# An attention layer on one core: the sum over head groups made in DRAM by accumulating transfers

## The chip, the cores and the metric

The kernel runs on one core of a Trainium2 chip. A core has TensorE (matrix products, written PE in the profile, its weight loads PEld), VectorE (DVE), ScalarE (ACT), GpSimd (POOL) and SyncE (SP), which here only issues transfers. The engines run on their own instruction streams and wait for each other through semaphores. SP and ACT issue transfers to hardware queues, GpSimd to a software queue; all of them are carried out by the same 16 DMA engines. The metric is the device time of one execution in microseconds (us).

## What is computed

```python
# x: (1, 2048, 512); 16 heads, q/k of 128+64, v of 128; latent of 384 for q, 128 for k and v
def attn(x, w_qa, q_ln, w_qb, w_kva, kv_ln, w_kvb, w_o):
    q = rms_norm(x @ w_qa.T, q_ln) @ w_qb.T        # per head: 128 plain, 64 rotated
    ckv = x @ w_kva.T                              # 128 latent, 64 rotated key part
    kv = rms_norm(ckv[..., :128], kv_ln) @ w_kvb.T
    scores = causal(q_full @ k_full.T * 192 ** -0.5)
    return merge_heads(softmax(scores) @ v) @ w_o.T
x = layernorm(x + attn(x, ...))
x = layernorm(x + x @ (weight * scale_weight[:, None]).T + bias)
```

## The kernel before

The program has three phases, with a barrier of all engines between them.

The **first phase** (up to 162 us) folds the weights, projects the tokens and leaves their latent forms in SBUF and DRAM. Its last transfer on the SP queue copies the input `x` into a DRAM tensor `y_dram` of 16 tiles (128 tokens by 512 outputs each). So `y_dram` starts as the residual, and the attention phase adds the attention's output to it.

The **attention phase** (162 to 1811 us) runs over 64 turns, numbered `it`: 4 groups of 4 heads (`G`), and in each group the 16 tiles of 128 queries, in the order of `PAIR_ORDER`. A turn of query tile `n` has `keys(it)` = n + 1 key tiles, from 1 to 16, together 544. For each key tile TensorE makes the scores of 4 heads (`scores`, 5 products), ScalarE copies them to a ring in SBUF (`copy_scores`), VectorE keeps the running maximum (`max_of`), later subtracts it (`shift`), ScalarE takes the exponent (`exp`) and its rounded part (`hi`), VectorE adds up the sum (`add_up`), GpSimd makes the rest of the split (`values_lo`, L1282), and TensorE multiplies with the values (`values`). After a turn's last key tile come the step of the sum (`turn_sum`, `reduce_sum`, `spread_sum`), `normalise` on VectorE, the split of the output into `o_t` (`out_hi` on ScalarE, `out_lo` on GpSimd, L1287) and the product with the group's part of the output weights (`project_out`, 12 products, L1148, semaphore `y_ready`). It leaves a tile of 128x512 in one of three shared PSUM banks.

This tile has to be added to `y_dram`. In the kernel before, SP loads the tile of `y_dram` into one of two halves of the SBUF tensor `y` (`load_y`, L959), VectorE adds the PSUM bank to it (`add_y`, L1338, semaphore `y_added`), and SP stores it (`store_y`, L963). Since each tile is summed once in each of the 4 groups, `next_y` makes the load of the next turn wait until the last store has landed (`y_stored`). The PSUM bank is free for the next use when the add is done (`wait_read`). At the end of a group SP also loads the next group's output weights (`wo`, L974), behind the store in its program.

The order of all steps is made ahead of time by `timetable()` and `plan()`. The timetable gives each step a slot (one slot is one key tile) and a phase inside it; `e` is the slot of a turn's last `values`, and `("y", it)` stands at slot e + 4. What reads a shared bank (`readers`) comes one slot later, in phase READ. `plan()` lists the steps in this order, pulls ahead what `waits_for` names, and every engine runs through the list and takes its own kinds of step. So an instruction that waits holds up all that stands behind it on its engine.

After the list, GpSimd issues the loads for the **last phase** (1811 to 1906 us): the second layer's weights (L1304, 1024 KB), their scales (L1305) and the first 10 of the 16 finished tiles of `y_dram` (L1309). Those 12 transfers stand ahead of the barrier; behind it SP loads the last 6 tiles (L1509) and GpSimd the bias (L1535, L1537). The last phase takes the statistics of each tile, normalises, multiplies by the second weights, adds the bias and residual, normalises again and writes the output.

Of the kernel before, what the change touches and what calls it, by code (L numbers as in the profile page):

```python
# [53 lines left out]
class Memory:  # L54


    def __init__(self, nc, ctx):
# [26 lines left out]

        self.y_stored = ctx.enter_context(nc.semaphore("y_stored"))
# [9 lines left out]
def prepare_phase(nc, m, x, w_qa, w_kva, w_qb, w_kvb, w_o, q_ln, kv_ln, ident_in, mask_in, cos_in, sin_in):  # L95
# [6 lines left out]
    with ExitStack() as ctx:  # L102
# [114 lines left out]
        def _(sp):  # L217
# [12 lines left out]
            sp.dma_start(m.y_dram.rearrange("t p d -> (t p) d"), x).then_inc(m.y_stored, 16)  # L230
# [412 lines left out]
def timetable():  # L643

    for it in range(N_ITER):
# [17 lines left out]
        yield e + 4, USE_AT, ("y", it)  # L663
    for it in range(-2, N_ITER - 2):
        ahead = [("q", it // 2 + 1, 2 * (it % 2) + j) for j in range(2)]
        following = [("pe", it + 3)] if it + 3 < N_ITER and not opens_group(it + 3) else []
        if opens_group(it + 2):
            order = [("pe", it + 2), *ahead, ("turn_pe", it + 2), *following]
        else:
            order = [("turn_pe", it + 2), *following, *ahead]  # L670
        for j, use in enumerate(order):
            yield (window_slot(it, min(j, 3)) if it >= 0 else it), USE_AT, use


def readers(use):
# [13 lines left out]
    if use[0] == "y":  # L689
        return [("add_y", use[1])]  # L690
# [14 lines left out]
def waits_for(step):  # L705
# [70 lines left out]
    elif what == "add_y":  # L776
        yield ("y", it)
    elif what == "q_hi":
# [76 lines left out]
def attention_phase(nc, m, w_ffn, scale_w):  # L855


    with ExitStack() as ctx:
# [30 lines left out]
        y_loaded = [sem(f"y_loaded{n}") for n in range(2)]  # L889
        y_stored = m.y_stored  # L890
        y_added = sem("y_added")
# [65 lines left out]
        def _(sp):  # L957
            def load_y(o):
                sp.dma_start(y[:, o % 2, :], m.y_dram[tile_of(o)]).then_inc(y_loaded[o % 2], 16)  # L959

            def store_y(o):
                sp.wait_ge(y_added, o + 1)
                sp.dma_start(m.y_dram[tile_of(o)], y[:, o % 2, :]).then_inc(y_stored, 16)  # L963

            def next_y(o):
                if o + 1 < N_ITER and tile_of(o + 1) != tile_of(o):
                    sp.wait_ge(y_stored, 16 * (o + 1))
                    load_y(o + 1)
                store_y(o)
                if o + 1 < N_ITER and tile_of(o + 1) == tile_of(o):  # L970
                    sp.wait_ge(y_stored, 16 * (o + 2))
                    load_y(o + 1)
                if o % NT == NT - 1 and o + 1 < N_ITER:
                    sp.dma_start(words(m.wo), m.wo_dram[group(o)]).then_inc(wo_loaded, 16)  # L974
# [21 lines left out]
            sp.wait_ge(y_stored, 16)  # L996
            load_y(0)
            load_tokens(1)
            for what, *at in STEPS:
                if what in ("q", "pe"):  # L1000
                    next_tokens((what, *at))
                elif what == "y":
                    next_y(*at)
            sp.wait_ge(y_stored, 16 * (N_ITER + 1))
# [5 lines left out]
        def _(pe):  # L1010
            def wait_read(u):
# [7 lines left out]
                elif u[0] == "y":  # L1019
                    pe.wait_ge(y_added, u[1] + 1)  # L1020
# [157 lines left out]
        def _(act):  # L1178
# [53 lines left out]

            def out_hi(it):
# [5 lines left out]
            for what, *at in STEPS:  # L1239
# [14 lines left out]
                elif what == "copy_sum":  # L1254
                    copy_sum(*at)
                elif what == "o_hi":
                    out_hi(*at)

        @block.gpsimd
        def _(pool):  # L1260
# [23 lines left out]

            def out_lo(it):
# [3 lines left out]

            for what, *at in STEPS:  # L1290
# [6 lines left out]
                elif what == "o_lo":  # L1297
                    out_lo(*at)

# [7 lines left out]
            pool.wait_ge(y_stored, 16 * (N_ITER - NT + Y_FIRST + 1))  # L1307
# [4 lines left out]
        def _(dve):  # L1312
# [21 lines left out]

            def add_y(it):
                dve.wait_ge(y_ready, it + 1)
                dve.wait_ge(y_loaded[it % 2], 16 * (it // 2 + 1))
                nc.vector.tensor_tensor(y[:, it % 2, :], aux(("y", it)), y[:, it % 2, :], ALU.add).then_inc(y_added, 1)  # L1338
# [63 lines left out]
            for what, *at in STEPS:  # L1402
# [4 lines left out]
                elif what == "add_y":  # L1407
                    add_y(*at)
# [301 lines left out]
```

## Time and profile before

| | |
|---|---|
| median of 3 runs | 1909.88 us (1907.77 to 1910.48) |
| the profiled execution | 1907.47 us |
| its span, first to last instruction | 1905.8 us |
| busy share of the span: TensorE | 92% |
| VectorE | 74% |
| ScalarE | 59% |
| GpSimd | 52% |
| mean DMA rate over the span | 66 GB/s |

The profile is of one execution. Its own time (1907.47 us) is 1.7 us over the span, for what lies around the first and the last instruction, and 2.4 us below the median of the runs; what is worked out from it is laid on the median at the end. A row of a timeline gives the start and the duration in us, the engine, the line of the program, the operation, output and inputs, and in brackets how long the engine had been idle and what released it. "SPq" and "POOLq" are the queues' own instructions. Busy shares are means over stages with different limits.

### The profile page before, as it was taken

To read this page: it belongs to the slowest core of one execution; us is meant where nothing else is said; L and a number is where in the kernel's file an instruction comes from. 1 tells how busy PE (TensorE), PEld (TensorE's weight loads), DVE (VectorE), ACT (ScalarE), POOL (GpSimd) and SP (SyncE) were. 2 spreads that over 40 slices of the span, in tenths; PEclk is the share of its full clock that TensorE was granted. 3 is DMA by queue.
4 is the path that set the end of the run, shared out by engine and by line. 5 is a ranking of instruction groups with operands and counts; after the bars stand their busy time and mean duration, and the time that the engine had idled before them with its cause. 6 is when DMAs were issued, how large, how long until landed. Compare 5 with 4: busy or idle time off the path is not lost. (4 is left out here: it accounts for less than half of the span.)

```text
span 1905.8 us, 28136 instructions
## 1 busy us (share of the span) xinstructions
PE 1756.6 (92%) x8977; PEld 1415.6 (74%) x8977; DVE 1401.1 (74%) x2659; ACT 1129.1 (59%) x2247; POOL 988.6 (52%) x971
## 2 busy tenths in 40 slices
PE   5997899999999999999989999999999999998586
PEld 3565788888878778788877788887787878886442
DVE  1553588787878778878777688878788888877266
ACT  2553366666666666667556566666667667666220
POOL 2321255555555555555555465655556656556455
PEclk9998999999999999999999999999999999999899
DMA  7774101111111201010211101111111010100321
GB/s 229 296 307 165 39 18 34 45 34 45 67 40 40 82 14 56 23 56 12 85 43 66 58 22 45 34 45 67 40 40 67 28 39 34 34 23 23 122 72 56
DMA packets 56488, 125.96 MB, mean 66 GB/s; under 512 B 8800, under 2 KB 30560, under 8 KB 53984
## 3 DMA queue, kind: packets, MB, share of 16 engines
q1 hardware_dynamic: 47776, 76.56, 11.8%
q0 software_dynamic: 6848, 23.60, 3.7%
q10 hardware_dynamic: 1728, 24.12, 3.0%
q8 instruction: 69, 1.13, 0.2%
q14 instruction: 67, 0.55, 0.1%
HBM read 79.17 MB, written 49.28 MB: 67 GB/s over the span
## 5 line engine op out<-in xcount | busy, mean ns | idle before, releaser
L1282 POOL TENSOR_TENSOR split_p<-pool,split_p 128x512 fp32r<-128x512 f32 x544 | 704.6, 1296 | 524.1 <-ACT split_p L1219 523.8
L1088 PE MATMUL rows<-q_c,key_c 128*128 128x512 f32 x1632 | 480.5, 402 | 15.4 <-DVE top L1357 7.9
L1357 DVE TENSOR_TENSOR top<-rows,top 128x512 f32<-128x512 f32 x420 | 288.6, 687 | 188.1 <-ACT pool L1207 184.0
L1372 DVE TENSOR_TENSOR pool<-bank,pool 128x512 f32<-128x512 f32 x544 | 370.4, 681 | 22.3 <-PE bank L1106 21.9
L1207 ACT COPY pool<-rows 128x512 f32<-128x512 f32 x480 | 282.6, 589 | 144.7 <-PE rows L1088 143.5
L1212 ACT ACTIVATE pool<-pool 128x512 f32<-128x512 f32 x544 | 346.8, 638 | 36.0 <-DVE pool L1372 34.9
L1088 PE MATMUL rows<-q_pe,key_pe 128*128 128x512 f32 x1088 | 337.8, 392 | 0.0
L1219 ACT CAST split_p<-pool 128x512 fp32r<-128x512 f32 x544 | 333.3, 613 | 0.0
L1384 DVE TENSOR_TENSOR bank<-bank,pool 128x512 f32<-128x512 f32 x480 | 331.1, 690 | 0.0
L1088 PEld LDWEIGHTS rows<-q_c,key_c 128*128 128x128 f32 x1632 | 282.2, 189 | 62.8 <-DVE top L1357 14.2
L1088 PEld LDWEIGHTS rows<-q_pe,key_pe 128*128 128x128 f32 x1088 | 204.3, 188 | 46.3
L1116 PE MATMUL bank<-split_p,val 128*128 128x512 f32 x544 | 214.9, 395 | 7.3 <-ACT o_sum L1225 6.0
L1119 PE MATMUL bank<-split_p,val 128*128 128x512 f32 x544 | 215.0, 395 | 3.6 <-POOL split_p L1282 3.4
L1117 PE MATMUL bank<-split_p,val 128*128 128x512 f32 x544 | 212.3, 390 | 0.0
L1148 PE MATMUL rows<-wo,o_t 128*128 128x512 f32 x516 | 130.1, 402 | 22.4 <-POOL o_t L1287 22.3
L1189 ACT CAST rot<-rot_cos 128x256 fp32r<-128x256 f32 x64 | 26.0, 406 | 192.8 <-POOL rot_cos L1271 192.8
L1148 PEld LDWEIGHTS rows<-wo,o_t 128*128 128x128 f32 x516 | 97.0, 192 | 51.9 <-issue 31.8
L1287 POOL TENSOR_TENSOR o_t<-o_sum,o_t 128x512 fp32r<-128x512 f32 x64 | 82.5, 1290 | 90.5 <-ACT o_t L1237 90.3
L1116 PEld LDWEIGHTS bank<-split_p,val 128*128 128x128 f32 x544 | 102.1, 188 | 35.9 <-ACT o_sum L1225 12.2
L1119 PEld LDWEIGHTS bank<-split_p,val 128*128 128x128 f32 x544 | 102.1, 188 | 33.5 <-POOL split_p L1282 12.5
L1047 PE MATMUL rows<-cq,wq 128*128 128x256 f32 x837 | 118.3, 287 | 0.1
L1117 PEld LDWEIGHTS bank<-split_p,val 128*128 128x128 f32 x544 | 102.2, 188 | 21.3
(161 smaller groups left out, 2252.1 us busy)
## 6 DMA issues: line engine op xcount, KB each, us to landing
cq<-cq_dram SPq DMA_DIRECT2D x28, 768.0 KB, 4.9
y<-y_dram SPq DMA_DIRECT2D x64, 256.0 KB, 2.8
y_dram<-y SPq DMA_DIRECT2D x64, 256.0 KB, 2.0
wq_dram<-wq ACTq DMA_DIRECT2D x4, 2304.0 KB, 11.6
wo_dram<-wo ACTq DMA_DIRECT2D x4, 2048.0 KB, 10.5
wq<-wq_dram SPq DMA_DIRECT2D x3, 2304.0 KB, 8.6
cq_dram<-cq ACTq DMA_DIRECT2D x4, 1536.0 KB, 12.1
wo<-wo_dram SPq DMA_DIRECT2D x3, 2048.0 KB, 8.1
```

Of the source, the lines that this page charges most:

```text
L1088: mm = pe.matmul(by_head(out), k, q, start=(z == 0), stop=(z == 4))
L1116: pe.matmul(OUT, m.val[:, 0, j, :], split_p[:, n % 3, 0, :], start=(t == 0), stop=False)
L1117: pe.matmul(OUT, m.val[:, 1, j, :], split_p[:, n % 3, 0, :], start=False, stop=False)
L1119: pe.matmul(OUT, m.val[:, 0, j, :], split_p[:, n % 3, 1, :], start=False, stop=(t == keys(it) - 1)).then_inc(values_done, 1)
L1148: mm = pe.matmul(aux(u), o_t[:, a, h * P:h * P + P], m.wo[:, b, h, :], start=(n == 0), stop=(n == 3 * HG - 1))
L1207: nc.scalar.copy(slot(n), SCORES[n % N_SCORES]).then_inc(scores_copied, 1)
L1212: nc.scalar.activation(slot(n), slot(n), ACT.Exp).then_inc(exp_done, 1)
L1219: nc.scalar.copy(split_p[:, n % 3, 0, :], slot(n)).then_inc(p_hi, 1)
L1282: nc.gpsimd.tensor_tensor(split_p[:, n % 3, 1, :], slot(n), stored(split_p[:, n % 3, 0, :]), ALU.subtract).then_inc(p_lo, 1)
L1357: nc.vector.tensor_tensor(out, SCORES[n % N_SCORES], slot(number(it, 0)) if t == 1 else out, ALU.max).then_inc(scores_maxed, 1)
L1372: nc.vector.tensor_tensor(slot(n), MAXES, slot(n), ALU.add).then_inc(shifted, 1)
L1384: nc.vector.tensor_tensor(TOTAL, TOTAL, slot(n), ALU.add).then_inc(summed, 1)
```

## The change

The sum is made in DRAM. ScalarE copies the finished PSUM tile to `y` (`copy_y`), and GpSimd issues a transfer that adds this half of `y` to the tile in `y_dram` (`store_y`, with `accum_op=ALU.add`). VectorE's `add_y`, SP's 64 loads of `y` and SP's 64 stores are gone. Two accumulating transfers are never in flight together: each waits on GpSimd until the one before has landed. `copy_y` of turn `it` waits until the transfer of turn `it` - 2 has landed, since it writes to the same half. The bank is free when the copy is done. The loads of the output weights now wait on SP only for the group's last product.

```diff
-            sp.dma_start(m.y_dram.rearrange("t p d -> (t p) d"), x).then_inc(m.y_stored, 16)
+            sp.dma_start(m.y_dram.rearrange("t p d -> (t p) d"), x).then_inc(m.y_started, 16)
 ...
         yield e + 4, USE_AT, ("y", it)
+        yield e + 4 + 2, MAX, ("store_y", it)
 ...
-        return [("add_y", use[1])]
+        return [("copy_y", use[1])]
 ...
-    elif what == "add_y":
+    elif what == "copy_y":
         yield ("y", it)
+        if it >= 2:
+            yield ("store_y", it - 2)
+    elif what == "store_y":
+        yield ("copy_y", it)
 ...
-            def load_y(o):
-                sp.dma_start(y[:, o % 2, :], m.y_dram[tile_of(o)]).then_inc(y_loaded[o % 2], 16)
-            def store_y(o):
-                sp.wait_ge(y_added, o + 1)
-                sp.dma_start(m.y_dram[tile_of(o)], y[:, o % 2, :]).then_inc(y_stored, 16)
 ...
+            def next_wo(o):
+                sp.wait_ge(y_ready, o + 1)
+                sp.dma_start(words(m.wo), m.wo_dram[group(o)]).then_inc(wo_loaded, 16)
 ...
-                    pe.wait_ge(y_added, u[1] + 1)
+                    pe.wait_ge(y_copied, u[1] + 1)
 ...
+            def copy_y(it):
+                act.wait_ge(y_ready, it + 1)
+                if it >= 2:
+                    act.wait_ge(y_stored, 16 * (it - 1))
+                nc.scalar.copy(y[:, it % 2, :], aux(("y", it))).then_inc(y_copied, 1)
 ...
+            def store_y(it):
+                pool.wait_ge(y_copied, it + 1)
+                if it:
+                    pool.wait_ge(y_stored, 16 * it)
+                pool.dma_start(m.y_dram[tile_of(it)], y[:, it % 2, :], accum_op=ALU.add).then_inc(y_stored, 16)
 ...
-            def add_y(it):
-                dve.wait_ge(y_ready, it + 1)
-                dve.wait_ge(y_loaded[it % 2], 16 * (it // 2 + 1))
-                nc.vector.tensor_tensor(y[:, it % 2, :], aux(("y", it)), y[:, it % 2, :], ALU.add).then_inc(y_added, 1)
```

The order of TensorE's work stays as it was, and so does that of all other steps on the other engines; only the steps named here go, come or change engine. Three places show it. In the rows, a part in brackets names the semaphores that the instruction waits for.

GpSimd at the end of the attention phase, from turn 59 on, before (`o_t` is `out_lo`, `split_p` is `values_lo`):

```order
L1287 TENSOR_TENSOR o_t<-o_sum,o_t 128x512 [waits o_hi]
L1282 TENSOR_TENSOR split_p<-pool,split_p 128x512 [waits p_hi] x4
L1287 TENSOR_TENSOR o_t<-o_sum,o_t 128x512 [waits o_hi]
L1282 TENSOR_TENSOR split_p<-pool,split_p 128x512 [waits p_hi] x2
L1287 TENSOR_TENSOR o_t<-o_sum,o_t 128x512 [waits o_hi] x3
L1304 DMA pool<-in_L_ffn_weight 128x4x512 [waits summed,p_lo]
L1305 DMA small<-in_L_ffn_scale_weight 128x4x1
L1309 DMA pool<-y_dram 128x512 [waits y_stored]
L1309 DMA pool<-y_dram 128x512 x9
L858 UNCONDITIONAL_BRANCH
```

and now:

```order
L1293 TENSOR_TENSOR o_t<-o_sum,o_t 128x512 [waits o_hi]
L1281 TENSOR_TENSOR split_p<-pool,split_p 128x512 [waits p_hi] x2
L1293 TENSOR_TENSOR o_t<-o_sum,o_t 128x512 [waits o_hi]
L1289 DMA y_dram<-y 128x512 [waits y_stored,y_copied]
L1293 TENSOR_TENSOR o_t<-o_sum,o_t 128x512 [waits o_hi] x2
L1289 DMA y_dram<-y 128x512 [waits y_stored,y_copied] x3
L1313 DMA pool<-in_L_ffn_weight 128x4x512 [waits summed,p_lo]
L1314 DMA small<-in_L_ffn_scale_weight 128x4x1
L1318 DMA pool<-y_dram 128x512 [waits y_stored]
L1318 DMA pool<-y_dram 128x512 x9
L864 UNCONDITIONAL_BRANCH
```

The accumulating transfer of turn 60 stands between the `out_lo` of turns 61 and 62, those of turns 61, 62 and 63 between the last `out_lo` and the 12 loads for the last phase.

SP where the third group of heads starts (turns 31 and 32), before:

```order
L959 DMA y<-y_dram 128x512 [waits y_stored]
L963 DMA y_dram<-y 128x512 [waits y_added]
L974 DMA wo<-wo_dram 128x4096
L959 DMA y<-y_dram 128x512 [waits y_stored]
L963 DMA y_dram<-y 128x512 [waits y_added]
```

and now:

```order
L980 DMA wq<-wq_dram 128x4608 [waits projected]
L970 DMA cq<-cq_dram 128x6x256 [waits projected] x2
L965 DMA wo<-wo_dram 128x4096 [waits y_ready]
L970 DMA cq<-cq_dram 128x6x256 [waits projected] x5
L980 DMA wq<-wq_dram 128x4608 [waits projected]
```

The output weights no longer stand behind a store that waits for VectorE's add.

ScalarE in turn 59's part without scores (`split_p` is `hi`, ACTIVATE is `exp`), before:

```order
L1237 CAST o_t<-o_sum 128x512 [waits y_ready,normalised]
L1212 ACTIVATE pool<-pool 128x512 [waits shifted]
L1219 CAST split_p<-pool 128x512 [waits values_done,exp_done]
L1212 ACTIVATE pool<-pool 128x512 [waits shifted]
L1219 CAST split_p<-pool 128x512 [waits values_done,exp_done]
L1212 ACTIVATE pool<-pool 128x512 [waits shifted]
L1219 CAST split_p<-pool 128x512 [waits values_done,exp_done]
```

and now:

```order
L1234 CAST o_t<-o_sum 128x512 [waits y_ready,normalised]
L1202 ACTIVATE pool<-pool 128x512 [waits shifted]
L1209 CAST split_p<-pool 128x512 [waits values_done,exp_done]
L1202 ACTIVATE pool<-pool 128x512 [waits shifted]
L1209 CAST split_p<-pool 128x512 [waits values_done,exp_done]
L1228 COPY y<-rows 128x512 [waits y_stored,y_ready]
L1202 ACTIVATE pool<-pool 128x512 [waits shifted]
L1209 CAST split_p<-pool 128x512 [waits values_done,exp_done]
```

The copy of turn 58 stands ahead of an exponent and a rounding that did not wait for the product.

## Rows read from the trace of the kernel before

**Rows 1.** Table by stretch; engine busy us (instructions), granted clock, DMA share, GB/s
```profile
core 0: us, PE busy (x) PEld busy (x) DVE busy (x) ACT busy (x) POOL busy (x), PEclk, DMA share, GB/s
...
200.00:1700.00 1500.00, 1450.52 (x7586) 1212.06 (x7587) 1191.70 (x2131) 979.41 (x1903) 830.48 (x743) 1.00 0.13 43
```

**Rows 2.** Waits of TensorE, 200 to 1780 us: total us, times, longest us
```profile
PE rows L1148 <- POOL o_t L1287: 16.3, 20, 1.7
PE rows L1088 <- DVE top L1357: 7.9, 10, 2.0
PE bank L1148 <- POOL o_t L1287: 7.1, 9, 1.7
```

**Rows 3.** Groups of instructions; busy us, mean ns, idle before it, releasers
```profile
L1225 ACT COPY o_sum<-bank 128x512 f32<-128x512 f32 x64 | 37.9, 592 | 10.0 <-PE bank L1119 4.5 <-POOL o_t L1287 3.4
```

**Rows 4.** Waits of VectorE for TensorE ahead of the adds, whole program
```profile
DVE y L1338 <- PE rows L1148: 26.6, 22, 6.1
...
DVE y L1338 <- PE bank L1148: 6.6, 8, 3.5
```

**Rows 5.** Timeline around the add of turn 6; start, duration, [idle before]
```profile
401.30 0.69 DVE L1338 TENSOR_TENSOR y<-bank,y 128x512 f32<-128x512 f32 x1 [0.68 <-PE bank L1148]
...
402.43 0.59 ACT L1207 COPY pool<-rows 128x512 f32<-128x512 f32 x1 [2.70 <-PE rows L1088]
```

**Rows 6.** Timeline, start of the attention phase
```profile
171.12 0.35 SPq L959 DMA_DIRECT2D y<-y_dram  x1
...
176.49 1.84 PE L1059 MATMUL rows<-wq,cq 128*128 128x256 f32 x7 [2.32 <-DMA cq<-cq_dram]
```

**Rows 7.** Timeline where the third group of heads starts
```profile
1040.91 0.69 DVE L1338 TENSOR_TENSOR y<-rows,y 128x512 f32<-128x512 f32 x1 [0.20 <-PE rows L1148]
...
1042.00 0.43 SPq L974 DMA_DIRECT2D wo<-wo_dram  x1
...
1050.50 4.57 PE L1148 MATMUL bank<-wo,o_t 128*128 128x512 f32 x12 [3.98 <-issue]
```

**Rows 8.** Timeline, turns 58 and 59, after the last scores
```profile
1741.71 0.63 ACT L1212 ACTIVATE pool<-pool 128x512 f32<-128x512 f32 x1
...
1745.73 0.69 DVE L1338 TENSOR_TENSOR y<-rows,y 128x512 f32<-128x512 f32 x1 [4.26 <-PE rows L1148]
...
1767.49 0.68 DVE L1338 TENSOR_TENSOR y<-rows,y 128x512 f32<-128x512 f32 x1
...
1769.13 0.62 PE L1135 MATMUL rows<-ident,sums 128*128 128x128 f32 x4 [1.49 <-DVE sums L1391]
```

**Rows 9.** DMA issues; count, KB each, median us from issue to landing
```profile
y<-y_dram SPq DMA_DIRECT2D x64, 256.0 KB, 2.8
y_dram<-y SPq DMA_DIRECT2D x64, 256.0 KB, 2.0
...
out_dram<-o_out POOLq DMA_DIRECT2D x16, 256.0 KB, 2.4
```

**Rows 10.** Timeline, end of the attention phase and start of the last
```profile
1794.82 0.79 POOL L1304 DMA_DIRECT2D pool<-in_L_ffn_weight  x1
...
1796.35 5.33 POOL L1309 DMA_DIRECT2D pool<-y_dram  x10
1799.65 0.69 DVE L1338 TENSOR_TENSOR y<-rows,y 128x512 f32<-128x512 f32 x1 [6.08 <-PE rows L1148]
...
1811.77 0.54 POOL L1535 DMA_DIRECT2D bias_rows<-in_L_ffn_bias  x1 [10.09 <-POOLq L858]
```

**Rows 11.** GpSimd's last load before the barrier, issued 1801.1
```profile
L1309 POOL DMA_DIRECT2D pool<-y_dram x1: 539/539/539, 1801.1 to 1801.1; - x1
...
DMA to landing us min/median/max: 9.4/9.4/9.4
```

**Rows 12.** Waits of the SP queue, 1790 to 1812 us
```profile
SPq L858 <- PEq L858: 2.9, 1, 2.9
```

**Rows 13.** Chain that ended last, 1790 to 1822: start us, us, what
```profile
1812.30 6.60 DMA bias_rows<-in_L_ffn_bias
```

More of the change, by code:

```diff
@@ L83, in __init__ @@
         self.wo_dram = nc.dram_tensor("wo_dram", (G, P, 2 * HG * HID), F32, kind="Internal").ap()
+        self.y_started = ctx.enter_context(nc.semaphore("y_started"))
         self.y_stored = ctx.enter_context(nc.semaphore("y_stored"))
@@ L888, in attention_phase @@
         cq_loaded = sem("cq_loaded")
-        y_loaded = [sem(f"y_loaded{n}") for n in range(2)]
         y_stored = m.y_stored
-        y_added = sem("y_added")
+        y_copied = sem("y_copied")
         y_ready = sem("y_ready")
@@ L957, in _ @@
         def _(sp):
-            def load_y(o):
-                sp.dma_start(y[:, o % 2, :], m.y_dram[tile_of(o)]).then_inc(y_loaded[o % 2], 16)
-            def store_y(o):
-                sp.wait_ge(y_added, o + 1)
-                sp.dma_start(m.y_dram[tile_of(o)], y[:, o % 2, :]).then_inc(y_stored, 16)
[L965 to L974, printed above, removed]
+            def next_wo(o):
+                sp.wait_ge(y_ready, o + 1)
+                sp.dma_start(words(m.wo), m.wo_dram[group(o)]).then_inc(wo_loaded, 16)
             def load_tokens(s):
@@ L995, in _ @@
             sp.wait_ge(m.cq_free, 16 * (NCH + 1))
-            sp.wait_ge(y_stored, 16)
-            load_y(0)
             load_tokens(1)
@@ L1001, in _ @@
                     next_tokens((what, *at))
-                elif what == "y":
-                    next_y(*at)
-            sp.wait_ge(y_stored, 16 * (N_ITER + 1))
+                elif what == "y" and at[0] % NT == NT - 1 and at[0] + 1 < N_ITER:
+                    next_wo(*at)
+            sp.wait_ge(y_stored, 16 * N_ITER)
             sp.wait_ge(cq_loaded, 16 * CQ_COUNT[-1])
@@ L1257, in _ @@
                     out_hi(*at)
+                elif what == "copy_y":
+                    copy_y(*at)
         @block.gpsimd
@@ L1288, in out_lo @@
                                         ).then_inc(o_lo, 1)
+            pool.wait_ge(m.y_started, 16)
             for what, *at in STEPS:
@@ L1298, in _ @@
                     out_lo(*at)
+                elif what == "store_y":
+                    store_y(*at)
             last = N_ITER - 4
@@ L1306, in _ @@
                            allow_slow_non_contiguous=True).then_inc(m.ffn_w_loaded, 16)
-            pool.wait_ge(y_stored, 16 * (N_ITER - NT + Y_FIRST + 1))
+            pool.wait_ge(y_stored, 16 * (N_ITER - NT + Y_FIRST))
             for u in range(Y_FIRST):
@@ L1406, in _ @@
                     q_rest(*at)
-                elif what == "add_y":
-                    add_y(*at)
                 elif what == "max" and at[1] == 0:
```

## The prediction

> **What bounds the kernel now.** I read the table by stretch first. Between 200 and 1700 us TensorE is busy 1450.5 of 1500 us, at the full granted clock, while VectorE has 1191.7, ScalarE 979.4 and GpSimd 830.5 [rows 1]. TensorE's work is not touched, so this stretch can give at most its 49.5 us of gaps. The second view is who ends those gaps: GpSimd's `out_lo` 29 times (16.3 + 7.1 us), VectorE's running maximum 10 times (7.9 us) [rows 2]. The rest of the program (start, the end of the attention phase, the last phase) runs on chains, and there each step counts in full.
>
> **ScalarE's copies.** 64 copies from PSUM. The nearest row, also a 128x512 copy from PSUM to SBUF, takes 592 ns [rows 3]: 37.9 us of work. On the path, most cost nothing. Ahead of 30 of the 64 adds VectorE stood waiting for TensorE to finish the product (22 + 8 times) [rows 4], and ScalarE is in the same state: after turn 6's product (ready at 401.3) its next instruction began at 402.43 after 2.70 us of idling [rows 5]. The copy fits into this hole. What covers it is that TensorE makes the next scores meanwhile; without them the copy would cost 0.6 us.
>
> **VectorE's adds.** They go: 64 x 0.69 = 44 us of work [rows 5]. But an add that starts the moment the product ends, on an engine that waited, held nothing up. Bounds: nothing, or at most the 39 waits of rows 2, each shortened by one add, in the 34 turns of 64 where VectorE did not wait ahead of it: 39 x 0.69 x 34/64 = 14.3 us. I take 0.5 us in the loop, near the lower end, because `out_lo` is late mostly for its own chain (normalise, round, rest, one behind the other on three engines), in which no add stands.
>
> **SP.** With the first `load_y` gone (0.35 us of issue) the token load behind it starts that much earlier, and TensorE waited 2.32 us for this load [rows 6]: -0.35. Where the third group of heads starts, the product of turn 32 waited 3.98 us; the load of its weights was issued at 1042.00, and the product of turn 31, which it now waits for, was ready at 1040.91 [rows 7]: -1.1. The other SP transfers move earlier and nobody waits for them.
>
> **Turns 58 and 59**, where no scores are left. ScalarE ran `exp` at 1741.71, and the product of turn 58 ended at 1745.73 [rows 8]. Now the copy stands ahead of that `exp`: up to 4.0 us later. ScalarE idled afterwards anyway because VectorE's `shift` stood behind the add, and this `shift` now comes early; what stays late is one rounding and GpSimd's work behind it. Bounds 0 and +4.0, taken +0.5. A turn later the add at 1767.49 stood ahead of `reduce_sum`, for which TensorE waited 1.49 us [rows 8]: -0.7, one add.
>
> **GpSimd's issues.** One issue takes 0.54 us (ten in 5.33 us) [rows 10], 64 are 34.6 us; all of it a loss if they lay on the path. GpSimd has 670 us free in the loop [rows 1] and each issue stands behind a `values_lo` that is needed a slot later: 0.
>
> **How long an accumulating transfer takes** (P, from issue to the next one's release) the trace does not show. From below: a plain store from GpSimd of the same 256 KB, 2.4 us. From above: load and store one after the other, 2.8 + 2.0 = 4.8 us [rows 9]. I take the middle, P = 3.6, since it reads DRAM as well but overlaps the two. The Trainium skill (DMA: Bandwidth & Descriptors, Anatomy of one DMA — SWDGE (gpsimd) path) fits a software-queue transfer as about 2.0 us plus the bytes over 436 GB/s, an estimate of 2.6 us for this size; the plain store's 2.4 us agrees, and no row shows whether it holds with an add. By that rule the end below would come out as in rival B.
>
> **The end of the attention phase** is the large term. Before, the 12 loads for the last phase were issued from 1794.82, right behind the last `out_lo`, while TensorE still worked on the last product (its add began at 1799.65) [rows 10]. Now three accumulating transfers stand ahead of them. Turn 61's goes out at 1794.9. Turn 62's waits for it, turn 63's for both and for the copy (1799.65 + 0.6 = 1800.3). So the last goes out at max(1800.3, 1794.9 + 2P) = 1802.1, and the loads follow at 1802.6 instead of 1794.82: 7.8 us late. Does it matter? Everything of the last phase hangs behind the barrier. GpSimd's last load was issued at 1801.14 and landed 9.4 us later, at 1810.5 [rows 11]; SP, whose own store had landed, waited 2.9 us more [rows 12]; the barrier opened 0.7 us after that landing (first instruction behind it on GpSimd at 1811.77, bias) [rows 10]. I read that GpSimd does not pass the barrier before its own transfers have landed. Then the landing moves with the issue. SP's last store no longer competes, about one load's pace, -0.5. So the barrier opens 7.8 - 0.5 = 7.3 us later, and the chain behind it begins with the bias load (6.60 us) [rows 13], which is issued after the barrier and shifts in full. Term: +7.3; with P = 2.4 it is +5.5, with P = 4.8 +9.7.
>
> **The sum.** -0.35 - 1.1 - 0.5 + 0.5 - 0.7 + 7.3 = +5.15 us. On the profiled execution's 1907.47 that is 1912.6; on the median 1909.88, 1915.0.
>
> **Rivals.**
> A, the forecast: P between 3 and 5.5, all steps as above; 1913 to 1919.
> B, P at its lower end: the copy of turn 63 sets the last issue. -2.15 + 5.5 = +3.35, 1913.2. For it: the plain store's 2.4 us. Against it: the extra read.
> C, the barrier does not wait for landings. Then it opens about when before, and the first statistics, which need all ten tiles, start when the last has landed, 1810.5 + 7.3 = 1817.8. With some 3.5 us of statistics and normalising behind that, the first use of the bias comes at 1821.3 instead of at the bias's landing, 1812.3 + 6.6 = 1818.9: +2.4 - 2.15 = about 0, 1910. For it only that releasers are inferred; against it rows 11 and 12.
> D, the other side: VectorE's relief reaches TensorE. The place is `normalise` ahead of `out_lo` and the maxima ahead of scores; price -14.3 instead of the -1.2 for adds: 5.15 - 13.1 = -8, 1901.9. It decides from some 6 us of gain in the loop. For it: VectorE is second in load, 79% [rows 1]. Against it: rows 4 and 5.
> E, accumulating is slow, P about 8: the last issue at 1810.9, +16 at the end, and GpSimd blocked between the close transfers of the short turns 31 to 33, some 3 us: -2.15 + 19 = +17, 1927. Nothing in the profile excludes it.
>
> **How the numbers follow.** A 0.55, B 0.15, C 0.08, D 0.12, E 0.10. About 0.2% (3.8 us) is what a measurement of this kernel can tell from no change. B, C and a tenth of A lie within it (0.28), D is faster (0.12), the rest of A and E slower (0.60). Likeliest is A: 1915.0 us. The range takes in C and B below and P = 5.5 with 2 us of slips in the loop above: 1907.5 to 1922; outside are D and E's upper part.
>
> **What would show it.** Between 200 and 1700 us TensorE's gaps stay within 2 us of 49.5. The gap ahead of turn 32's product shrinks from 4.0 to about 2.9. The accumulating transfers land 3 to 5 us after issue, the last is issued some 7 us behind the last `out_lo`, and the bias load is issued 7 us later, counted from the last product. The last phase keeps its length behind the barrier. I am wrong if the bias load is issued at the same distance as before (C), if TensorE's gaps in the loop fall by more than 6 us (D), or if GpSimd stands waiting for landings in the middle of the loop (E).

## The result, and the profile of the changed kernel

| | before | changed |
|---|---|---|
| time, median (lowest to highest) | 1908.22 us (1906.43 to 1910.48, 6 runs) | 1917.24 us (1915.67 to 1918.97, 6 runs) |
| ratio | | 1.0046, 95% interval 1.0033 to 1.0059 |
| profiled execution, span | 1905.8 us | 1914.9 us |

The change makes the kernel 9.0 us slower, 0.46%. The direction, the mechanism and the place were forecast (1915.0 us, slower). The size was not quite: +5.15 us forecast, +9.0 measured. Experiments below show which two terms of the end were off and which one was missing.

I read the changed kernel in the order in which the prediction read the other. First the table by stretch (busy us and instructions of each engine, granted clock, DMA share, GB/s), to be held against [rows 1]:

```profile
core 0: us, PE busy (x) PEld busy (x) DVE busy (x) ACT busy (x) POOL busy (x), PEclk, DMA share, GB/s
...
200.00:1700.00 1500.00, 1452.89 (x7598) 1212.87 (x7596) 1159.82 (x2082) 1013.06 (x1964) 878.11 (x803) 1.00 0.14 33
```

VectorE lost 32 us of work there, ScalarE got 34 and GpSimd 48. TensorE's gaps went from 49.5 to 47.1 us. Second, TensorE's waits from 200 to 1780 us (total us, times, longest), against [rows 2]:

```profile
PE rows L1138 <- POOL o_t L1293: 17.1, 20, 1.7
PE rows L1078 <- DVE top L1361: 7.8, 10, 2.0
PE bank L1138 <- POOL o_t L1293: 7.0, 9, 1.7
...
PE bank L1138 <- issue: 3.0, 1, 3.0
```

Three rows stand as they stood (16.3, 7.9 and 7.1 us before). TensorE waits for GpSimd's `out_lo` and VectorE's running maximum as long as ever: the 44 us that VectorE was spared went past them. The last row is the wait for the third group's weights, 3.98 us in [rows 7]. The timeline there (start, duration, [idle before]):

```profile
1037.76 0.33 SPq L965 DMA_DIRECT2D wo<-wo_dram  x1
1037.77 0.58 ACT L1228 COPY y<-rows 128x512 f32<-128x512 f32 x1 [0.75 <-PE rows L1138]
...
1040.85 0.86 POOL L1289 DMA_DIRECT2D y_dram<-y  x1
...
1046.42 4.28 PE L1138 MATMUL bank<-wo,o_t 128*128 128x512 f32 x12 [3.05 <-issue]
```

The load of `wo` goes out at 1037.76, at the moment at which the copy of turn 31 starts; before it went out 1.09 us behind the start of turn 31's add. The wait shrinks to 3.05 us. Third, the accumulating transfers in the table of DMA issues (count, KB each, median us from issue to landing), against the first two of [rows 9]:

```profile
y_dram<-y POOLq DMA_DIRECT2D x64, 256.0 KB, 4.1
```

And the same transfers by their tile, from 200 to 1700 us: who waited for them (us in total, times), and the times to landing:

```profile
  POOL y_dram L1289: 6.7, 4
...
DMA to landing us min/median/max: 3.7/4.1/7.8
```

They land 4.1 us after issue, and the few that must wait for the one before do so for 6.7 us in 1500, on an engine that has time. Fourth, the end of the attention phase, against [rows 10]:

```profile
1790.89 0.85 POOL L1289 DMA_DIRECT2D y_dram<-y  x1
...
1795.64 0.85 POOL L1289 DMA_DIRECT2D y_dram<-y  x1 [3.90 <-DMA y_dram<-y]
1795.71 0.58 ACT L1228 COPY y<-rows 128x512 f32<-128x512 f32 x1 [5.62 <-PE rows L1138]
1800.25 0.84 POOL L1289 DMA_DIRECT2D y_dram<-y  x1 [3.75 <-DMA y_dram<-y]
1800.82 1.07 POOL L1313 DMA_DIRECT2D pool<-in_L_ffn_weight  x1
...
1802.38 5.61 POOL L1318 DMA_DIRECT2D pool<-y_dram  x10
...
1820.87 0.54 POOL L1537 DMA_DIRECT2D bias_rows<-in_L_ffn_bias  x1 [12.88 <-POOLq L864]
```

The three rows of L1289 are the transfers of turns 61, 62 and 63. Each of the last two was issued only after the one before had landed (idle 3.90 and 3.75 us "<-DMA y_dram<-y"); turn 63's copy (L1228, 1795.71) had been ready since 1796.29. Ten loads of the sum begin at 1802.38, before at 1796.35, and the bias load at 1820.87, before at 1811.77. GpSimd's last two loads by their tile (the last is the one of 9.9 us), against [rows 11]:

```profile
L1318 POOL DMA_DIRECT2D pool<-y_dram x2: 834/836/837, 1806.6 to 1807.2; - x2
...
DMA to landing us min/median/max: 8.8/9.3/9.9
```

Issued at 1807.16, the last load landed at 1817.04. GpSimd went on 3.83 us later; before it was 1.23 us (1810.54 to 1811.77). The chain that ended last begins, as in [rows 13], with the second bias load:

```profile
1821.40 6.71 DMA bias_rows<-in_L_ffn_bias
```

With these, the 9.1 us between the two spans divide like this (moments in us):

| | before | changed | difference |
|---|---|---|---|
| TensorE's first instruction of the attention phase | 162.45 | 160.36 | -2.1 |
| from there to the end of the last product | 1637.16 | 1635.31 | -1.9 |
| from `out_lo` of turn 63 to the first load of the 12 | -0.06 | 9.87 | +9.9 |
| from there to the last landing | 15.72 | 16.22 | +0.5 |
| from that landing to the bias load | 1.23 | 3.83 | +2.6 |
| from there to the end | 93.99 | 94.01 | 0 |

(The last product ends 4.7 us behind that `out_lo` in both.) The first line is not the change's: in the eleven traces of this study it lies between 160.3 and 162.5, and the ranges of the two kinds of kernel overlap (160.3 to 161.9 and 161.1 to 162.5).

### The profile page after: what moved, and what is told of

The parts are those of the page before. It is cut to its first block and busy times, and to the rows that moved or that the text cites. A ratio compares the mean times of both kernels' runs of the same rounds, so it can differ in the third digit from the quotient of the medians.

```text
span 1914.9 us, 28133 instructions
## 1 busy us (share of the span) xinstructions
PE 1755.8 (92%) x8977; PEld 1413.8 (74%) x8977; DVE 1360.6 (71%) x2595; ACT 1163.5 (61%) x2311; POOL 1038.9 (54%) x1035
## 5 line engine op out<-in xcount | busy, mean ns | idle before, releaser
L1281 POOL TENSOR_TENSOR split_p<-pool,split_p 128x512 fp32r<-128x512 f32 x544 | 712.9, 1316 | 481.3 <-ACT split_p L1209 480.7
L1078 PE MATMUL rows<-q_c,key_c 128*128 128x512 f32 x1632 | 480.8, 403 | 15.3 <-DVE top L1361 7.8
L1138 PE MATMUL rows<-wo,o_t 128*128 128x512 f32 x516 | 130.0, 402 | 21.8 <-POOL o_t L1293 21.7
## 6 DMA issues: line engine op xcount, KB each, us to landing
cq_dram<-cq ACTq DMA_DIRECT2D x4, 1536.0 KB, 12.3
```

The costliest lines, as they stand in the source:

```text
L1078: mm = pe.matmul(by_head(out), k, q, start=(z == 0), stop=(z == 4))
L1138: mm = pe.matmul(aux(u), o_t[:, a, h * P:h * P + P], m.wo[:, b, h, :], start=(n == 0), stop=(n == 3 * HG - 1))
L1281: nc.gpsimd.tensor_tensor(split_p[:, n % 3, 1, :], slot(n), stored(split_p[:, n % 3, 0, :]), ALU.subtract).then_inc(p_lo, 1)
```

## Experiments

Names: "the tail" is the time from the end of the last product to the issue of the bias load. It was 12.2 us before and is 25.2 us in the changed kernel.

**1. The 12 loads to SP, in the changed kernel.** They leave the end of GpSimd's program and stand at the end of SP's, which has nothing left to do there.

```diff
+            sp.wait_ge(y_stored, 16 * (N_ITER - NT + Y_FIRST))
+            for u in range(Y_FIRST):
+                sp.dma_start(all_sums(m)[:, u, :], m.y_dram[OUT_ORDER[u]]).then_inc(m.y_first_loaded, 16)
             sp.wait_ge(y_stored, 16 * N_ITER)
...
-            pool.wait_ge(y_stored, 16 * (N_ITER - NT + Y_FIRST))
-            for u in range(Y_FIRST):
-                pool.dma_start(all_sums(m)[:, u, :], m.y_dram[OUT_ORDER[u]]).then_inc(m.y_first_loaded, 16)
```

The two loads of weights ahead of these, with their waits, move in the same way.

> The changed kernel, with the 12 loads for the last phase (second weights, scales, ten finished tiles) issued by SP instead of GpSimd, so that they no longer stand behind the last three accumulating transfers and GpSimd has none of them outstanding at the barrier. In the changed kernel the last product ended at 1795.7, the last accumulating transfer landed at 1804.5, and the barrier opened at 1820.4. My theory (GpSimd passes the barrier only when its own transfers have landed, and the loads stand behind the chain of three): the barrier opens at 1805.2 to 1808, 12 to 15 us earlier than in the changed kernel, and the time is 1902 to 1905, below the kernel before by 3 to 6 us. Rival (the barrier is late for another reason, or the loads would land as late from SP): 1912 or more.

Measured: 1904.9 us (10 runs), ratio to before 0.998 (0.997 to 0.999), where the changed kernel stands at 1.0046. The loads were out from 1753.85 on. GpSimd's timeline at the end:

```profile
1803.27 0.84 POOL L1298 DMA_DIRECT2D y_dram<-y  x1 [3.77 <-DMA y_dram<-y]
...
1810.66 0.58 POOL L1537 DMA_DIRECT2D bias_rows<-in_L_ffn_bias  x1 [6.55 <-POOLq L864]
```

So the place of the loads behind the accumulating transfers was the cost, and the changed kernel with its loads moved is a little faster than the unaltered kernel before. The tail is 12.4 us: the chain of three transfers still stands in it (the last issued at 1803.27, landed at 1807.28), and then 3.4 us to the bias load, with no load outstanding that could explain them. The barrier came later than the 1808 that I had expected at the latest, but that moment was counted from a last product that ended at 1795.7; here it ended at 1798.3, and counted from there the barrier lies within the expectation (11.6 us to the end of GpSimd's drain, 9.5 to 12.3 expected).

**2. The same 12 loads to SP, in the kernel before,** behind the store of turn 60. This asks whether experiment 1 shows a merit of accumulating at all. In SP's program:

```diff
                 elif what == "y":
                     next_y(*at)
+                    if at[0] == N_ITER - 4:
...
+                        sp.wait_ge(y_stored, 16 * (N_ITER - NT + Y_FIRST + 1))
+                        for u in range(Y_FIRST):
+                            sp.dma_start(all_sums(m)[:, u, :], m.y_dram[OUT_ORDER[u]]).then_inc(m.y_first_loaded, 16)
```

> The kernel before, with the same 12 loads issued by SP, behind the store of turn 60; the sum is still made by VectorE and SP. It separates what the place of the loads is worth from what the accumulating transfers cost. My theory: the last add ends at about 1800.3, its store lands 2.0 us later with no load beside it, and the barrier opens 1 us behind that, at 1803 to 1804 instead of 1811.3: 1900 to 1902. The same rival as in the run beside it: no change, 1907 to 1909. If the first theory holds for both, this one is 2 to 4 us faster than the changed kernel with the loads on SP, for the chain of three accumulating transfers.

Measured: 1901.63 us (9 runs), ratio 0.9962 (0.9951 to 0.9973). The move itself is worth less here than in the changed kernel (6.6 us, there 12.3), but the kernel that it leaves is 3.3 us faster than that of experiment 1: with the loads moved in both, accumulating loses. Its timeline:

```profile
1796.61 0.69 DVE L1339 TENSOR_TENSOR y<-rows,y 128x512 f32<-128x512 f32 x1 [6.25 <-DMA y<-y_dram]
...
1806.38 0.59 POOL L1536 DMA_DIRECT2D bias_rows<-in_L_ffn_bias  x1 [9.42 <-POOLq L858]
```

There is a price: the loads lie beside the sum's own traffic, turn 61's store took 7.5 us (1789.70 to 1797.19), and VectorE's add of turn 62 waited 6.25 us for its load. The bias load came 0.9 us behind the landing of SP's last store (1805.48); GpSimd had nothing under way and had been ready since 1797.0.

**3. Plain stores in place of accumulating ones** (the sum over the groups is left out).

```diff
-                pool.dma_start(m.y_dram[tile_of(it)], y[:, it % 2, :], accum_op=ALU.add).then_inc(y_stored, 16)
+                pool.dma_start(m.y_dram[tile_of(it)], y[:, it % 2, :]).then_inc(y_stored, 16)
```

> The changed kernel with plain stores from GpSimd in place of accumulating ones: the additions are left out, all waits and the order stay. A plain store of this size from GpSimd landed in 2.4 us, an accumulating one in 4.1. My theory: two periods of 2.9 instead of 4.7 us ahead of the last one, which then goes out when its copy is done, some 3.6 us earlier, and the loads and the barrier with it: span 1914.9 - 3.6 = 1911.3. In the changed kernel GpSimd's drain ended 3.2 us behind its last landing, in the kernel before 0.6 us. If the accumulation makes this, it goes too: 1908.7. If the 64 further transfers from GpSimd make it, it stays: 1911.3.

Measured: one run, 1911.23 us, span 1909.5. The transfers of turns 61 and 62 now took 2.3 us each to land and that of turn 63 2.8 us; from issue to issue it was 2.84 us. So turn 63's waited for its copy alone:

```profile
1796.01 0.59 ACT L1228 COPY y<-rows 128x512 f32<-128x512 f32 x1 [5.61 <-PE rows L1138]
1796.88 0.54 POOL L1289 DMA_DIRECT2D y_dram<-y  x1 [2.32 <-ACT y L1228]
...
1798.94 5.32 POOL L1318 DMA_DIRECT2D pool<-y_dram  x10
...
1815.53 0.54 POOL L1537 DMA_DIRECT2D bias_rows<-in_L_ffn_bias  x1 [11.27 <-POOLq L864]
```

The last product ended at 1795.97, so the tail is 19.6 us, 5.6 less than with accumulating, where I had expected 3.6: 3.7 because the first load is issued 1.5 us behind the last product instead of 5.2, and 1.9 because the 12 loads then take 14.3 us from the first issue to the last landing instead of 16.2. The last load landed at 1811.70 and the bias load came 3.83 us later, exactly as with accumulating. That extra belongs to something else.

**4. The copy on VectorE instead of ScalarE,** all else as changed. It gives VectorE its load back.

```diff
-                act.wait_ge(y_ready, it + 1)
+                dve.wait_ge(y_ready, it + 1)
...
-                nc.scalar.copy(y[:, it % 2, :], aux(("y", it))).then_inc(y_copied, 1)
+                nc.vector.tensor_copy(y[:, it % 2, :], aux(("y", it))).then_inc(y_copied, 1)
```

> The changed kernel with the copy from PSUM on VectorE, at the place of the former add, and none on ScalarE. It gives VectorE back about the load that the change took away (0.6 to 0.7 us a turn) and takes it from ScalarE. My theory (VectorE's relief gives TensorE nothing in the loop): TensorE's busy time between 200 and 1700 us stays within 1 us of 1452.9 and the span within 1.5 us of 1914.9. Rival (VectorE's relief reaches TensorE, for 6 us or more in the loop): the span is 1921 or more.

Measured: one run, 1919.5 us, span 1917.8. TensorE was busy 1452.3 us between 200 and 1700, with the copy on ScalarE 1452.9, and the product that starts at 1688.9 there starts 1.3 us later here, counted from the first instruction of the phase: VectorE's relief is worth about 1 us in the loop. The span is 2.9 us longer, twice what I had allowed. Another 1.9 us came between 1737 and 1769. Of these, 0.6 us is the copy itself: on VectorE it again stands ahead of `reduce_sum`, and TensorE's wait for the sum is 1.49 us as in [rows 8], where the changed kernel has 0.89.

```profile
1769.05 0.62 PE L1125 MATMUL rows<-ident,sums 128*128 128x128 f32 x4 [1.49 <-DVE sums L1393]
```

For the rest the granted clock differs. Rows of TensorE alone (busy us, granted clock, DMA share, GB/s), first the changed kernel:

```profile
1740.00:1750.00 10.00, 7.63 (x29) 0.96 0.22 26
...
1760.00:1770.00 10.00, 7.29 (x41) 1.00 0.22 26
```

The same with the copy on VectorE:

```profile
1740.00:1750.00 10.00, 9.26 (x31) 0.76 0.21 26
...
1760.00:1770.00 10.00, 7.80 (x35) 0.83 0.00 0
```

In the two slices with 0.76 and 0.83 TensorE ran a part of the time at the lower of its two levels (1.2 instead of 2.4 GHz): the product of turn 59 took 4.53 us there instead of 2.99. Over 1730 to 1800 the shortfalls of the slices add up to 8.5 us here and 5.7 us in the changed kernel, 2.8 us apart. That is enough for what is left of the 1.9 us, but it is read from two single traces; what moved the clock was not tested.

**5. Turns 61 and 62 without their transfers** (that part of the sum is left out), so that turn 63's waits for its copy only. The waits for the two missing landings go with them.

```diff
             def store_y(it):
                 pool.wait_ge(y_copied, it + 1)
+                if it in (N_ITER - 3, N_ITER - 2):
+                    return
```

> The changed kernel without the transfers of turns 61 and 62, so that turn 63's waits for turn 60's alone (that part of the sum is missing from the output). Chain theory: in the changed kernel the last accumulating transfer was issued 9.3 us behind the last out_lo (two waits of 4.7 us); here it waits for the product and its copy only, some 5 us behind out_lo, and the 12 loads move up with it: the bias load is issued about 4 us earlier counted from the last product, 21 us instead of 25.2, span about 1911. If the end of GpSimd's drain does not follow the issue but something else (the number of transfers in the program, DRAM), it stays within 1 us of 25.2, span 1914 to 1915. GpSimd's drain should again end about 3.1 us behind its last landing; if the three accumulating transfers close behind each other made the extra 2.6 us, it is near 0.6 us.

Measured: one run, 1912.36 us, span 1910.7:

```profile
1796.31 0.86 POOL L1291 DMA_DIRECT2D y_dram<-y  x1 [5.96 <-ACT y L1228]
...
1816.92 0.54 POOL L1539 DMA_DIRECT2D bias_rows<-in_L_ffn_bias  x1 [12.82 <-POOLq L864]
```

The last product ended at 1795.08, so the tail is 21.8 instead of 25.2 us: -3.4 where 4 were expected. The chain of transfers is the cause of the late issue. The last landing was at 1813.17 and the bias load 3.75 us behind it: the extra at the barrier has nothing to do with three transfers close together.

**6 and 7. Small extra loads by GpSimd, in the kernel before:** 128x4 elements behind every `out_lo` (6), behind every second one (7). Each waits for the one before to land.

```diff
                 elif what == "o_lo":
                     out_lo(*at)
+                    if at[0]:
+                        pool.wait_ge(extra, 16 * at[0])
+                    pool.dma_start(spare, w_ffn[0:P, 0:4]).then_inc(extra, 16)
```

> The kernel before with one small extra load (128x4) issued by GpSimd behind every out_lo, 64 in all, each waiting for the one before. Tells apart two readings of why GpSimd left the barrier 0.54 us behind its last landing in the kernel before and 3.15 us in the changed one. Count reading: what matters is that GpSimd issued some 64 transfers more; then the drain ends about 3.1 us behind the last landing here too, and the span is some 3 us longer than before (1908 to 1910). Store reading: what matters is that GpSimd stored to DRAM; then the drain ends about 0.6 us behind the last landing and the span is 1905 to 1908.

> The kernel before with 32 small extra loads by GpSimd, one behind every second out_lo. So far GpSimd's drain at the barrier ended behind its last landing by 0.54 us with 12 transfers issued since the last barrier, 2.66 with 64, 3.06 with 74 and 3.15 with 76: some 0.04 us for each. Line theory: 44 transfers give 1.8 us. Step theory (a fixed 3 us once the count passes some bound): about 0.5 or about 3 us.

Measured: spans of 1909.1 us in both, one run each (1910.7 and 1910.8 us). With 64 extra loads, GpSimd's last two loads by their tile (the last has the largest figure), and the bias load in the timeline:

```profile
L1315 POOL DMA_DIRECT2D pool<-y_dram x2: 537/538/539, 1802.0 to 1802.5; - x2
...
DMA to landing us min/median/max: 7.9/8.4/9.0
```

```profile
1815.32 0.54 POOL L1541 DMA_DIRECT2D bias_rows<-in_L_ffn_bias  x1 [12.26 <-POOLq L858]
```

With 32, the same two views:

```profile
L1316 POOL DMA_DIRECT2D pool<-y_dram x2: 537/538/539, 1802.6 to 1803.2; - x2
...
DMA to landing us min/median/max: 7.8/8.4/9.1
```

```profile
1814.78 0.54 POOL L1542 DMA_DIRECT2D bias_rows<-in_L_ffn_bias  x1 [11.09 <-POOLq L858]
```

With 64 more, the last landing was at 1811.49 and the bias load 3.83 us later; with 32 more, 1812.25 and 2.53 us. Beside the other kernels, ordered by the number of transfers that GpSimd issued in the attention phase (the phase ahead of it is the same in all):

| transfers by GpSimd | 12 | 44 | 64 | 64 | 74 | 76 | 76 | 76 | 76 |
|---|---|---|---|---|---|---|---|---|---|
| kernel | before | 7 | 1 | 9 (below) | 5 | changed | 3 | 4 | 6 |
| last landing to bias load, us | 1.23 | 2.53 | 3.38 | 3.38 | 3.75 | 3.83 | 3.83 | 3.83 | 3.83 |

That is a line: 0.73 us and 0.041 us for each transfer, whether it loads or stores, adds or not, is 2 KB or 256 KB. The forecast for 44, made from the others, came out as written. 64 transfers more are 2.6 us, to be paid once at the barrier. The trace has a record of GpSimd's drain, the instruction that ends its part of a phase: it ends 0.54 us behind the last landing before and 3.15 us in the changed kernel, and the bias load follows 0.7 us behind it in both. What GpSimd does in that time no row shows.

The line is read at this barrier, and the slope is not the same elsewhere. At the first barrier (41 transfers by GpSimd, the last landed 15.5 us or more before the drain began) the drain takes 4.17 us in all eleven traces; at this one it takes 1.38 us where GpSimd had issued nothing in the phase (experiments 2 and 8). So the count matters even when all has long landed, by 0.07 us for each transfer there. At the end of the last phase, with 18 transfers, the drain ends 1.78 us behind the last landing, where the line would give 0.8. It does so in all eleven, though GpSimd's transfers since the start of the program are 59 in some and 135 in others: the count starts again with each phase.

**8. The kernel before with the loads placed better.** The 12 loads on SP ahead of its entry for turn 59, where SP idles, and the weights of the next group of heads loaded as early as in the changed kernel: in `next_y` their load now stands ahead of `store_y(o)`.

```diff
                     load_y(o + 1)
+                if o % NT == NT - 1 and o + 1 < N_ITER:
+                    sp.wait_ge(y_ready, o + 1)
+                    sp.dma_start(words(m.wo), m.wo_dram[group(o)]).then_inc(wo_loaded, 16)
                 store_y(o)
...
                 elif what == "y":
+                    if at[0] == N_ITER - 5:
...
                     next_y(*at)
```

> The kernel before (VectorE adds, SP loads and stores the sum), with the 12 loads issued by SP ahead of its entry for turn 59, where they fall into SP's idle time from about 1754, and with the weights of the next group of heads loaded as soon as the product has been made, as in the changed kernel. Theory: GpSimd has nothing outstanding at the barrier, SP's stores of turns 61 to 63 run alone (2.0 us instead of 7.5 for turn 61's), so SP's last store goes out behind turn 63's add and lands 2 to 3 us later: barrier some 0.5 to 2 us earlier than with the loads behind turn 60's store, and the gap ahead of turn 32's product 3.0 instead of 4.0 us. Median 1898.5 to 1901, against 1901.6 there. Rival: TensorE or the engines of the attention phase lose to the loads beside turns 58 and 59, then 1901.5 or more.

Measured: 1900.67 us (4 runs), ratio 0.9948 (0.993 to 0.9967). The tail is 3.6 us, near what an add, a store of 2.0 us and the barrier need. What the early load of `wo` brought is less clear. The timeline there, and behind it the load by its tile:

```profile
1042.79 0.33 SPq L971 DMA_DIRECT2D wo<-wo_dram  x1
...
1043.52 0.32 SPq L963 DMA_DIRECT2D y_dram<-y  x1
...
1052.45 3.75 PE L1159 MATMUL bank<-wo,o_t 128*128 128x512 f32 x8 [4.04 <-issue]
```

```profile
DMA to landing us min/median/max: 9.6/9.6/9.6
```

It was issued 1.1 us sooner behind the product and took 9.6 us. The wait is 4.04 us, against the trace of before (8.4 us and 3.98) no gain. But that load is the shortest of those issued in the old order: in experiments 2, 6 and 7, which keep this order, it took 9.3, 9.6 and 9.0 us, and TensorE waited 4.84, 5.11 and 4.60 us. Against these the earlier issue would be worth 0.6 to 1.1 us; single traces do not decide it. In the six kernels that send the sum over GpSimd the load took 8.0 to 8.6 us and the wait was 2.5 to 3.05 us. In the changed kernel turn 30's transfer runs beside the load (1040.85, 3.1 us behind it), and turn 31's goes out at 1052.72, when the load has landed; in the kernels with VectorE's adds turn 31's store runs beside it. That this is why the load is shorter was not tested.

**9. The changed kernel without its chain.** The loads on SP as in 1, and one landing semaphore for each buffer of `y`. An accumulating transfer now waits for the one before only where both add to the same tile. All of the reference is computed.

```diff
-                if it:
-                    pool.wait_ge(y_stored, 16 * it)
-                pool.dma_start(m.y_dram[tile_of(it)], y[:, it % 2, :], accum_op=ALU.add).then_inc(y_stored, 16)
+                if it and tile_of(it) == tile_of(it - 1):
+                    pool.wait_ge(landed[(it - 1) % 2], 16 * ((it - 1) // 2 + 1))
+                pool.dma_start(m.y_dram[tile_of(it)], y[:, it % 2, :], accum_op=ALU.add
+                               ).then_inc(landed[it % 2], 16)
```

> The changed kernel with the 12 loads issued by SP (as the run after_sp_loads) and with one landing semaphore for each of the two buffers of y, so that an accumulating transfer waits for the one before only where both add to the same tile. Everything is computed. Chain theory: the last accumulating transfer is issued right behind the copy of turn 63, 0.7 us behind the last product, lands 4.1 us later, GpSimd's drain ends 2.7 us behind that, and the bias load is issued 8 to 8.5 us behind the last product instead of 12.4: median 1900 to 1902, as good as the kernel before with its loads on SP (1900.7). Rival: close accumulating transfers slow each other (they lie less than 4.1 us apart in the last turns and at the change of groups) or the drain grows, and the tail keeps more than 11 us: 1904 or more.

Measured: 1900.12 us (6 runs), ratio 0.9955 (0.994 to 0.997):

```profile
1792.33 1.74 POOL L1300 DMA_DIRECT2D y_dram<-y  x2
...
1796.48 0.58 ACT L1240 COPY y<-rows 128x512 f32<-128x512 f32 x1 [4.95 <-DMA y_dram<-y]
1797.36 0.84 POOL L1300 DMA_DIRECT2D y_dram<-y  x1 [3.29 <-ACT y L1240]
...
1804.65 0.58 POOL L1540 DMA_DIRECT2D bias_rows<-in_L_ffn_bias  x1 [6.45 <-POOLq L865]
```

Turns 61 and 62 go out in one row (x2). The copy of turn 63 waited for turn 61's buffer ("<-DMA y_dram<-y", landed 1796.40) and not for the product, which had ended at 1795.54; hence a tail of 9.1 us instead of the 8 to 8.5 expected. Two overlapping accumulating transfers took 4.1 and 5.5 us.

So the idea can be had as a gain of 0.45%. The old way of summing, with its loads moved (experiment 8), reaches the same (0.52%, intervals overlapping).

## Why the prediction was partly right, point by point

**What bounds the loop.** Right. That VectorE's relief does not reach TensorE (rival D refuted) is shown by the waits above and by experiment 4 (which also takes the copy off ScalarE): about 1 us of the loop, where 6 would have been needed.

**VectorE's adds and the loop's other terms.** Forecast -2.15 us for everything between first and last product, measured -1.9. That agreement is in part luck: over all traces, the five with VectorE's adds have 1637.2 to 1640.6 us there and the five that send the sum over GpSimd and copy on ScalarE 1633.7 to 1638.0, in the mean 4.3 us less. The trace that I predicted from was the shortest of its kind, though the other four carry extra or moved loads, one trace each. The medians of six runs point the same way: they lie 9.0 us apart, and the tail's 13.0 leaves -4.0 for all that comes ahead of it. Between 200 and 1700 us TensorE is busy 1448.7 to 1450.5 us in the first five and 1452.1 to 1453.0 in all six that send the sum over GpSimd, 3.1 us more in the mean. My bound "within 2 us of 49.5" for the gaps just failed (47.1). Most of this stays when VectorE copies (4) and all of it when nothing is accumulated (3). That speaks for the sum's loads and stores that left SP's queue, and against VectorE's load, but no run tests it. The wait at turn 32 is 1.7 us of the 4.3, in the mean of the same traces; where the rest comes from was not separated.

**SP at the start.** Forecast -0.35. The token load landed 0.4 us sooner, counted from the first instruction of the phase, and TensorE's wait for it fell from 2.32 to 1.38 us. **Turn 32:** forecast -1.1, measured -0.93. Over all traces the wait is 4.0 to 5.1 us with VectorE's adds and 2.5 to 3.05 without; how much of that is the earlier issue, experiment 8 leaves open.

**Turns 58 and 59.** The gap that should shrink by one add, 1.49 us in [rows 8], is 0.89 us, -0.6 for the -0.7 forecast. TensorE waited 1.14 us for GpSimd's `split_p` at 1746.5, the late rounding that was put at +0.5. That was too little: from the start of turn 58's product to this step of the sum it is 28.6 us, before 27.9, so the two terms together are +0.7 where -0.2 was forecast. With -0.6 for the gap, the late rounding is worth about +1.3.

```profile
1746.49 0.50 PE L1109 MATMUL bank<-split_p,val 128*128 128x512 f32 x1 [1.14 <-POOL split_p L1281]
...
1765.38 0.62 PE L1125 MATMUL rows<-ident,sums 128*128 128x128 f32 x4 [0.89 <-DVE sums L1395]
```

**ScalarE's copies and GpSimd's issues at 0.** They held: from 200 to 1700 us TensorE waited 19.7 us for `out_lo` (20.3 before) and 2.6 us for ScalarE's `o_sum` (3.5 before). ScalarE idled for the product ahead of 45 of 57 copies.

**How long an accumulating transfer takes.** This is the mis-sized term. Taken was P = 3.6, the middle between a plain store (2.4) and load and store one behind the other (4.8). Measured from issue to issue: 4.75 and 4.61 us. Two things were too small. The landing took 4.1 to 4.2 us, between the two rows. And both rows were times to landing, while P runs to the next issue, which came 0.5 us behind each landing, with plain stores too (2.84 us for landings of 2.3, experiment 3). Two of them stand in the chain, 2 x 1.1 = 2.2 us. By the prediction's own formula, max(1800.3, 1794.9 + 2 x 4.68) = 1804.3, and the loads are then 9.9 us late, as measured. The Trainium skill's rule (DMA: Bandwidth & Descriptors, Anatomy of one DMA — SWDGE (gpsimd) path), estimated at 2.6 us, fits the plain stores of experiment 3 (2.3, 2.3 and 2.8 us) and not the accumulating ones (4.1 us).

**The landing distance.** Forecast -0.5 for SP's missing store, measured +0.5 (16.22 for 15.72). With plain stores it was -1.4 (14.3, experiment 3). So SP's store was worth more than I took, and an accumulating transfer still under way ahead of the loads costs 1.9 us that I had not counted; 1.0 us is left against the forecast. These are differences of single traces: this distance is 15.3 us in experiment 4 and 16.3 in 5, both with an accumulating transfer ahead, and 15.3 and 15.4 in experiments 6 and 7.

**"Then the landing moves with the issue" and the barrier with the landing.** The first half held, and rival C fell: the bias load moved with the landing. The second half lacked a term. From landing to barrier I took the 0.7 us of the kernel before as the barrier's own and constant. In the rows it is 1.23 us from the landing to the bias load; 0.7 is the part behind the drain, which does stay. The part ahead of it grows with the number of transfers that GpSimd has issued: +2.6 us. No row of before could show it, since only one such number stood at this barrier; the step that failed is to have carried a distance over to a kernel in which GpSimd issues six times as many transfers.

The tail in sum: 7.3 forecast, 13.0 measured = 7.3 + 2.2 (P) + 1.0 (landing) + 2.6 (count), less 0.1 of rounding. **Rival E**, GpSimd blocked in the loop, did not come: 6.7 us of waiting there, harmless.

## What to carry to other kernels

An engine's last transfers before a barrier are on the path in full, each with everything queued behind it: before a small transfer is moved to another queue, read what is issued behind it there, and move that out first (here worth 12 us in the changed kernel and 7 to 10 us in the one before). A chain of transfers that wait for each other's landing is priced by its period times its length, and need not exist where they touch different tiles. An engine that is relieved on the average but was waiting at the places in question gives little back (here about 1 us of 44).

## What the runs showed that I had not expected

- GpSimd left the barrier behind the attention phase later by 0.041 us for every transfer it had issued in the phase: 1.23, 2.53, 3.38, 3.75, 3.83 us from last landing to next instruction for 12, 44, 64, 74 and 76 transfers. The other two barriers have the effect with other numbers (4.17 us of drain for 41 transfers long landed). With none under way from GpSimd (experiments 2 and 8), its drain ended long before SP's last landing and the first instruction came 0.9 us behind that.
- An accumulating transfer of 256 KB from SBUF to DRAM takes 4.1 us where a plain one from the same queue takes 2.3 to 2.4, and 6.6 us beside the load of 2 MB at turn 32.
- In the rows, issues in kernels that accumulate last 0.84 us instead of 0.54, the loads behind them too, but the next instruction begins 0.57 us behind the start (1800.25 to 1800.82): the engine is hardly held longer.
- A store of 256 KB by SP, 2.0 us when alone, took 7.5 us beside 12 loads and 9.5 us beside the load of 2 MB.
